# LSTM and RNN layers, step by step: a bias copy and four sums moved, one matmul group of the second half between the first half's

## What is computed

```python
def step(carry, xw_t):                  # first layer
    prev_h, prev_c = carry
    a = xw_t + prev_h @ Wh              # (16, 512) @ (512, 2048), xw_t = x_t @ Wx + b
    i, f, o = sigmoid(a[:, :H]), sigmoid(a[:, H:2*H]), sigmoid(a[:, 2*H:3*H])
    g = tanh(a[:, 3*H:])
    next_c = f * prev_c + i * g
    next_h = o * tanh(next_c)
...
def step(h, xw_t):                      # second layer, on x + first layer's output
    h_next = tanh(h @ Wh + xw_t)
...
x = x + lstm(x); x = x + rnn(x)
```

## Time and profile before

| | us |
|---|---|
| median of 3 runs | 2277.07 |
| lowest and highest | 2273.94, 2279.57 |
| the profiled execution | 2289.59 |
| its span | 2287.8 |
| TensorE busy | 2210.8 |
| VectorE busy | 2100.8 |
| ScalarE busy | 1782.7 |
| GpSimd busy | 116.1 |

### The profile page before, as it was taken

How to read it: one execution, slowest core, us unless ns; L and a number is a source line. 1 busy time by engine, 2 the same in 40 slices (tenths; PEclk the granted TensorE clock), 3 DMA queues, 4 the chain that set the end, 5 groups by cost and what they waited for, 6 DMA issues and landing times.

```text
span 2287.8 us, 148190 instructions
## 1 busy us (share of the span) xinstructions
PE 2210.8 (97%) x63548; PEld 1835.4 (80%) x63548; DVE 2100.8 (92%) x11050; ACT 1782.7 (78%) x6431; POOL 116.1 (5%) x143
## 2 busy tenths in 40 slices
PE   3899999999999999999999999999999999999996
PEld 1688888888888888888888888888888888888885
DVE  6899999999999999999998999899999999899997
ACT  3688787887887788777887788778887888778885
POOL 4000000000000000000000000000000000000000
PEclk7999999999999999999999999999999999999998
DMA  5000000000000000000000000000000000000000
GB/s 209 3 23 23 18 23 14 18 22 23 18 23 13 18 23 22 18 16 19 18 23 21 19 13 23 18 23 18 23 13 18 23 23 18 22 14 18 23 13 12
DMA packets 16733, 53.88 MB, mean 24 GB/s; under 512 B 2256, under 2 KB 2384, under 8 KB 14800
## 3 DMA queue, kind: packets, MB, share of 16 engines
q1 hardware_dynamic: 16080, 44.41, 5.4%
HBM read 27.62 MB, written 16.78 MB: 19 GB/s over the span
## 4 chain that ended last, share of the span: by engine, by line
PE 95%; DVE 2%; issue 1%; ACT 1%; DMA 1%; POOL 0%; SPq 0%; DVEq 0%; ACTq 0%; POOLq 0%
PE in_ps L244 24%; PE rnn_ps L244 22%; PE rec_first_ps L244 20%; PE rec_second_ps L244 19%; PE c_ps L244 10%; DVE wh_part L452 1%; DMA x_sb<-xT 1%; ACT wh_part L658 0%; DVE turned L483 0%; DVE wh_parts L452 0%; POOL x_sums L211 0%; ACT wh_parts L658 0%; DVE largest_slice L407 0%; ACT gates_cell L693 0%; DVE pre_sb L489 0%
## 5 line engine op out<-in xcount | busy, mean ns | idle before, releaser
L244 PE MATMUL rec_first_ps<-wh_part,h_parts 128*32 128x256 f16 x16352 | 561.2, 273 | 20.7 <-DVE h_parts L536 20.6
L244 PE MATMUL rec_second_ps<-wh_part,h_parts 128*32 128x256 f16 x16352 | 560.9, 273 | 0.1
L244 PEld LDWEIGHTS rec_first_ps<-wh_part,h_parts 128*32 128x32 f16 x16352 | 436.3, 96 | 59.5 <-issue 32.2
L244 PEld LDWEIGHTS rec_second_ps<-wh_part,h_parts 128*32 128x32 f16 x16352 | 469.0, 97 | 1.1 <-issue 0.3
L244 PE MATMUL in_ps<-wx_sums,x_sums 128*32 128x256 f32 x6096 | 417.3, 379 | 2.2 <-issue 1.2
L244 PEld LDWEIGHTS rnn_ps<-wx_sb,y 128*32 128x32 f32 x8192 | 249.7, 109 | 156.4 <-issue 126.8
L693 ACT ACTIVATE gates_cell<-gate_ps,unscale 128x128 f32<-128x128 f32 x511 | 187.9, 368 | 240.3 <-DVE gate_ps L489 237.9
L244 PE MATMUL rnn_ps<-wx_sb,y 128*32 128x128 f32 x8192 | 347.6, 275 | 13.0 <-issue 6.3
L244 PE MATMUL rnn_ps<-wh_parts,h_parts 128*32 128x256 f16 x8176 | 344.8, 274 | 8.2 <-DVE h_parts L571 8.2
L244 PEld LDWEIGHTS in_ps<-wx_sums,x_sums 128*32 128x32 f32 x6096 | 225.2, 110 | 92.7 <-issue 4.7
L244 PEld LDWEIGHTS rnn_ps<-wh_parts,h_parts 128*32 128x32 f16 x8176 | 249.9, 97 | 11.4 <-issue 8.5
(11 more groups left out here) (93 smaller groups left out, 3575.8 us busy)
## 6 DMA issues: line engine op xcount, KB each, us to landing
x_sb<-xT SPq DMA_DIRECT2D x32, 512.0 KB, 4.1
yT<-y SPq DMA_DIRECT2D x64, 256.0 KB, 2.4
wh_sb<-wh SPq DMA_DIRECT2D x5, 1024.0 KB, 9.0
wx_sb<-wx SPq DMA_DIRECT2D x5, 1024.0 KB, 14.4
b_sb<-b SPq DMA_DIRECT2D x1, 256.0 KB, 2.7
b_sb<-b SPq DMA_DIRECT2D x1, 64.0 KB, 11.6
h_first<-h0T SPq DMA_DIRECT2D x1, 32.0 KB, 11.3
```

Source lines behind the costliest of these rows:

```text
L244: last = nc.tensor.matmul(out[QUAD * q:QUAD * (q + 1)], states, weights(q), start=False, stop=True, tile_position=(0, QUAD * q), skip_grou ...
```

## The change

Three things are moved; no computation is added or taken out.

- ScalarE: `bias1` follows `seed1` instead of `tanh_cell(0)`. Its wait for `seed1_done` stays.
- GpSimd: the four sums of a chunk are made at c = 3, 4, 7, 8 instead of 3, 4, 5, 6, and each waits for `h0_ready[1]` of the step (the second half of the state that step t reads) instead of `rec0_done[0]`.
- TensorE: `recurrent0` issues the first group (k = 0, high part) of the second output half between the first output half's groups with k = 0, 1 and those with k = 2, 3. The wait for the second half's seed moves there with it; the wait for `h0_ready[1]` comes behind that group.

```diff
+STEPS_OF_X_SUMS = (3, 4, 7, 8)
...
             for t in range(STEPS):
                 v, c = divmod(t, CHUNK)
-                if 3 <= c < 7 and v + 1 < CHUNKS:
-                    pool.wait_ge(rec0_done[0], t + 1)
-                    sum_x(v + 1, c - 3)
+                if c in STEPS_OF_X_SUMS and v + 1 < CHUNKS:
+                    pool.wait_ge(h0_ready[1], t)
+                    sum_x(v + 1, STEPS_OF_X_SUMS.index(c))
...
             def recurrent0(t):
 
-                for half in range(HALVES):
-                    pe.wait_ge(seed0_done[half], t + 1)
+                def group(half, k, part):
                     cols = slice(half * COLSH, (half + 1) * COLSH)
-                    for k in range(SUB):
-                        if half == 0 and k % SUBH == 0:
-                            pe.wait_ge(h0_ready[k // SUBH], t)
-                        for part in range(2):
-                            last = tiles(rec0_ps(t, half), h0_parts[:, k], lambda q: wh0_part[part][:, k, q, cols])
-                    last.then_inc(rec0_done[half], 1)
+                    return tiles(rec0_ps(t, half), h0_parts[:, k], lambda q: wh0_part[part][:, k, q, cols])
+
+                pe.wait_ge(seed0_done[0], t + 1)
+                pe.wait_ge(h0_ready[0], t)
+                for k in range(SUBH):
+                    for part in range(2):
+                        group(0, k, part)
+                pe.wait_ge(seed0_done[1], t + 1)
+                group(1, 0, 0)
+                pe.wait_ge(h0_ready[1], t)
+                for k in range(SUBH, SUB):
+                    for part in range(2):
+                        last = group(0, k, part)
+                last.then_inc(rec0_done[0], 1)
+                for k in range(SUB):
+                    for part in range(0 if k else 1, 2):
+                        last = group(1, k, part)
+                last.then_inc(rec0_done[1], 1)
...
                 if 0 <= s < STEPS:
                     seed1(s)
+                if s >= 0 and s % 2 and s // 2 + 2 < PAIRS:
+
+                    act.wait_ge(seed1_done, s + 1)
+                    bias1(s // 2 + 2)
                 if t < STEPS:
                     gates(0, t)
                 if s >= 1:
@@
                     o_half(0, t)
                     gates(1, t)
                     tanh_cell(0, t)
-                if s >= 0 and s % 2 and s // 2 + 2 < PAIRS:
-
-                    act.wait_ge(seed1_done, s + 1)
-                    bias1(s // 2 + 2)
                 if t < STEPS:
                     o_half(1, t)
                     tanh_cell(1, t)
```

## The result

The changed kernel takes 2214.85 us (median of 4 runs, 2212.88 to 2215.98), before it is 2278.32 (4 runs): ratio 0.9724, 95% interval 0.9707 to 0.974. The forecast was 2227 us, so the change gained 63 us where 50 were expected.

A forecast was written before the change was run, and what follows sets the result against it. Odd steps were taken as bound by the bias copy, even ones just by the state's chain. -43 - 12 + 5 = -50 us on the profiled 2289.6, scaled to the median, gave 2227 us; range 2212 to 2256.

The forecast's parts named there:

- Part 1, the bias copy: ScalarE: moving the copy removes TensorE's 0.17 us wait before `input1` in odd steps; 43 us gained (bounds 38 and 51).
- Part 2, the sums: GpSimd: sums started earlier no longer slow VectorE's L561; 124 x 0.095 = 11.8 us gained (bounds nothing and all).
- the rival in which the sums still cost: VectorE transposes are held by GpSimd's sums, so only the bias copy's move gains: 2239 us; chance 0.10.
- the transpose L556 would be held: VectorE: L556 held up to the sum's end at 1161.26, first half's turn slips, 0.10 per sum: nothing gained.
- Part 3, the early group: TensorE: one second-half group between the first half's state halves gains nothing in undisturbed steps (bounds 0 and 0.02), costs 0.
- The slack: VectorE: the second half's turn waits for its own matmuls, leaving 0.05 us when the first half ends 0.11 later.
- the rival in which the later first half is passed on: The first half's 0.11 us delay passes on in full, 4.255 us per step: 2275, no change; chance 0.08.
- What does not shrink: 25 us of TensorE bursts without instructions, outside undisturbed steps, stay; they hide some removed wait, +5 us (bounds 0 and 12).
- outside time far from 25 us: Sign that the prediction is wrong: time outside undisturbed steps in the profile after is far from 25 us.
- From profile to median: Profiled execution, 2289.6 us, is 0.55% above the median 2277.07; its forecast 2239.6 is scaled in that ratio to 2227.
- The rival in which TensorE starves more at the faster pace: TensorE must get instructions 2% faster; the 25 us of stalls double: 2252 us; chance 0.14.
- The slower rival: TensorE drains at two more changes between `rec_first_ps` and `rec_second_ps` per step, 0.11 each: 4.365 us steps, 2329; chance 0.06.

The follow-up runs named there:

- four groups: The full change with four groups of the second output half between the state's halves instead of one: 2336.13 us (2 runs), ratio 1.0263 to the kernel before.

## Why the prediction was right, and where it was not

- **Part 1, the bias copy**: right. The wait of 0.17 went, and the state took its place as the next bound at 4.15, forecast 4.145 to 4.15. The even steps came down to it too (4.15 from 4.17), at the end of their bounds that I took.
- **Part 2, the sums**: right, 0.095 each to nothing; this also settles the rival in which the sums still cost. The alternative that the transpose L556 would be held is refuted by its 0.31 under the sum. The trigger did it, not the steps.
- **Part 3, the early group**: right that it gains and costs nothing in the full change. The slack was put at 0.05 and measured at 0.08 of the step, so the rival in which the later first half is passed on falls too. What I did not see is that the group on its own costs 13 us, through the sums' trigger: the step "the price: the first half ends 0.11 later" followed VectorE but not GpSimd, which also waits for `rec0_done[0]`. In the full change part 2 removes that wait.
- **What does not shrink**: wrong, and this is the missing 13 us. I took the 25 us outside undisturbed steps as fixed and even took 5 back. They shrank by about 10 on the medians (by 21 in the profiled pair). I had reasoned only that a stall can hide the wait, which would cost part of the gain; the runs show that the wait draws the stalls out, in kernels that have it they come in long bursts. The term was +5 and measured -10. The rest of the sum, -55, measured -53.5. The prediction named this as a sign of being wrong (outside time far from 25 us), and it came: 5.3 in the profile. That the total still came close to the forecast is owed to the small size of this term, not to its reasoning.
- **From profile to median**: the profiled execution of before lay 0.5% above the median, with 26 us outside undisturbed steps; those 11 us are probably stalls of the same kind, which is argued from what agrees between the traces and not seen in a trace. If so, the term varies from execution to execution of one kernel. The scaling itself moved the forecast by less than 1 us.

The rival in which TensorE starves more at the faster pace, with the 25 us doubled, falls with the full change itself: its steps are 2% shorter and its outside time is 4 us where before has 15. A small effect of the pace stays possible (1 us with four groups, at 4.40 a step). The slower rival falls with the undisturbed steps of the early group alone.

## What to carry to other kernels

When an engine's stream shows a gap only in the distance between the starts of two groups, look for the wait instruction ahead of it and for what stands in front of the awaited work in the other engine's order; here the copy, which ended 3.55 us into the step, now ends at 1.93. Before an instruction that signals is put later, list everyone who waits for that signal, also the engine that is busy 5% of the time. Stall time that looks random may depend on the waits of the kernel, so compare it between kernels before taking it as fixed.

## What was not expected of the hardware

TensorE's stream stops at times by itself, in all these kernels. In the change without the bias move, the even step at 985.74 takes 4.80 us; its unit matmuls stop between two matmuls of one group of instructions, where the profile shows nothing that either waits for:

```profile
987.49 1.07 PE L245 MATMUL in_ps<-wx_sums,x_sums 128*32 128x256 f32 x16
988.35 0.64 PE L245 MATMUL c_ps<-wx_sb,x_sb 128*32 128x256 f32 x7
989.32 0.38 PE L245 MATMUL c_ps<-wx_sb,x_sb 128*32 128x256 f32 x1 [0.33 <-issue]
989.45 0.90 PE L245 MATMUL rnn_ps<-wx_sb,y 128*32 128x128 f32 x24
```

The stops come back about every 57 steps: in the full change steps 64, 119, 180, 236, 292, 350, 407 and 462 are among the disturbed. That is a distance in steps and not in time: the bursts of before end at 55, 114, 170, 228, 284, 340, 396 and 453, though its steps are longer, and with four groups, at 4.40 us a step, nearly all of the outside time lies in the steps 292 to 295 and 462. So it goes with the place in the program.

The trace points to the supply of instructions. The page of the full change has a DMA queue that brings instructions, here with packets, MB and share of the engines' time; 8.24 MB in 503 packets are 16 KB each:

```profile
q8 instruction: 503, 8.24, 1.6%
```

By the packets' start times, in every kernel here each of the eight stretches of 57 steps from step 16 on has 56 of these packets. Nearly every step starts one; the place in the step at which it starts moves on until a step has none. In the full change steps 59, 117, 173, 229, 287, 343, 401 and 457 are of this kind (besides 170, 231 and 507), and the stops named above come two to seven steps behind them. In a burst of before the packets come unevenly: steps 209, 211, 213 and 215 start none, 210, 212, 214 and 216 two each. (The last column of the earlier trace rows is 7 GB/s in the disturbed step at 1207.07 and 4 in an undisturbed one.) This ties the stops to the instruction packets; whether TensorE stops because a packet is late, or asks for it later because it stopped, the traces do not show. In the full change the costliest such place takes 0.9 us in all; with a wait ahead of `input1` a burst can last for 15 to 21 steps and take up to 4.8 us, about half of it in even and half in odd steps. Why a wait in that place draws them out stays open.
